# A transformer layer on eight cores: more load semaphores, and two kinds of store moved from ScalarE's DMA queue to SyncE's

## The reference

```
x = x + attn(layernorm(x)) @ wo.T        # causal softmax attention, q,k,v = h @ wq.T, wk.T, wv.T
g = silu(layernorm(x) @ w_gate.T)
u = layernorm(x) @ w_up.T
x = x + (g * u) @ w_down.T
```

## Time and profile before

| | us |
|---|---|
| median of 3 runs | 2900.47 (2899.7 to 2901.21) |
| profiled execution, its own time | 2899.5 |
| span of its slowest core (core 4), first to last instruction | 2897.1 |
| spans of the 8 cores | 2885.8 to 2897.1 |
| PE busy | 2449.2 (85%) |
| DVE busy, ACT busy | 557.8 (19%), 551.4 (19%) |
| DMA, mean over the span | 68 GB/s |

### The profile page before, as it was taken

How to read it: one execution, slowest core, us unless ns; L and a number is a source line. 1 busy time by engine, 2 the same in 40 slices (tenths; PEclk the granted TensorE clock), 3 DMA queues, 4 the chain that set the end, 5 groups by cost and what they waited for, 6 DMA issues and landing times.

```text
span 2897.1 us, 32038 instructions; the slowest of 8 cores (2885.8 to 2897.1 us)
## 1 busy us (share of the span) xinstructions
PE 2449.2 (85%) x12352; PEld 1142.4 (39%) x12352; DVE 557.8 (19%) x978; ACT 551.4 (19%) x1090; POOL 169.2 (6%) x324
## 2 busy tenths in 40 slices
PE   2676788888888888859879999999999999797886
PEld 1233344444444444414334444444444444343333
DVE  4322233333333333303210001000000000000000
ACT  4433223232333333302310000000000000000000
POOL 0000000000000000010000000000000011111110
PEclk9988999999999999958889999999999999898998
DMA  5433211101010101073234444444444435555554
GB/s 171 114 105 80 44 18 20 22 16 22 16 23 15 23 15 23 1 145 117 80 80 80 73 79 74 79 75 79 75 78 75 78 62 76 113 76 110 87 99 94
DMA packets 61491, 196.36 MB, mean 68 GB/s; under 512 B 6944, under 2 KB 6944, under 8 KB 56096
## 3 DMA queue, kind: packets, MB, share of 16 engines
q0 software_dynamic: 46080, 134.24, 28.5%
q1 hardware_dynamic: 9504, 43.29, 4.7%
q10 hardware_dynamic: 5760, 16.78, 1.5%
HBM read 311.72 MB, written 16.78 MB: 113 GB/s over the span
## 4 chain that ended last, share of the span: by engine, by line
PE 79%; ACT 7%; DMA 6%; issue 4%; DVE 4%; ACTq 0%; DVEq 0%; POOL 0%; SPq 0%; POOLq 0%
PE psA L717 8%; PE psB L728 8%; PE psA L394 4%; PE psA L414 4%; PE psA L802 4%; PE psB L394 4%; PE psB L414 4%; PE psF L728 4%; PE psE L728 4%; PE psC L717 4%; PE psD L717 4%; PE psB L802 4%; PE psB L331 2%; PE psA L331 2%; ACT p_sb L459 2%
## 5 line engine op out<-in xcount | busy, mean ns | idle before, releaser
L459 ACT ACTIVATE p_sb<-psA,stats 128x1024 bf16<-128x1024 f32 (+3 forms) x128 | 132.4, 1034 | 558.4 <-PE psA L443 290.5
L717 PE MATMUL psA<-h_fm,wg 128*128 128x512 bf16 x1024 | 227.9, 381 | 9.0 <-DMA wg<-wg_t 9.0
L728 PE MATMUL psB<-h_fm,wu 128*128 128x512 bf16 x1024 | 226.2, 379 | 0.0
L717 PE MATMUL psC<-h_fm,wg 128*128 128x512 bf16 x512 | 194.0, 379 | 0.0
L717 PE MATMUL psD<-h_fm,wg 128*128 128x512 bf16 x512 | 194.0, 379 | 0.0
L728 PE MATMUL psE<-h_fm,wu 128*128 128x512 bf16 x512 | 194.0, 379 | 0.0
L728 PE MATMUL psF<-h_fm,wu 128*128 128x512 bf16 x512 | 194.0, 379 | 0.0
L802 PE MATMUL psB<-wd,hidden 128*128 128x512 bf16 x512 | 155.4, 384 | 22.7 <-DVE osb L816 22.6
L802 PE MATMUL psA<-wd,hidden 128*128 128x512 bf16 x512 | 154.4, 382 | 5.6 <-DVE osb L816 3.8
L526 DVE CAST pt<-psD 128x512 bf16<-128x512 f32 x192 | 115.7, 603 | 210.2 <-PE psD L513 210.2
L717 PEld LDWEIGHTS psA<-h_fm,wg 128*128 128x128 bf16 x1024 | 100.5, 98 | 131.0 <-issue 11.4
(11 more groups left out here) (124 smaller groups left out, 2986.0 us busy)
## 6 DMA issues: line engine op xcount, KB each, us to landing
wg<-wg_t POOLq DMA_DIRECT2D x64, 512.0 KB, 5.1
wu<-wu_t POOLq DMA_DIRECT2D x64, 512.0 KB, 5.1
wd<-wd_t POOLq DMA_DIRECT2D x128, 256.0 KB, 3.8
xt<-xkv SPq DMA_DIRECT2D x16, 1024.0 KB, 5.7
wqbuf<-wq_t POOLq DMA_DIRECT2D x16, 512.0 KB, 5.1
xt<-xq SPq DMA_DIRECT2D x8, 1024.0 KB, 10.2
wkbuf<-wk_t POOLq DMA_DIRECT2D x16, 512.0 KB, 5.7
wvbuf<-wv_t POOLq DMA_DIRECT2D x16, 512.0 KB, 5.7
```

What stands on the lines that cost most here:

```text
L459: t_exp = P.do("scalar", lambda e, s=s, slo=slo, shi=shi, sec=sec, sc_t=sc_t, sstat=sstat: e.activation(sb["p_sb"][:, P_OFF[s] + slo:P_OFF ...
L717: t_gmm = P.do("tensor", lambda e, hc=hc, c=c, half=half, par=par, gb=gb: e.matmul(bk(gb[half]), wg[par][:, c, :], sb["h2_fm"][:, c, half ...
L728: t_umm = P.do("tensor", lambda e, hc=hc, c=c, half=half, par=par, ub=ub: e.matmul(bk(ub[half]), wu[par][:, c, :], sb["h2_fm"][:, c, half ...
```

## The change

Three edits. The groups `ld` and `wld` get six semaphores in place of four. The store of `x2t` (L651) is started by SP and no longer by ACT. So is the store of `osb` (L821).

```diff
-DMA_GROUPS = {"ld": 4, "wld": 4, "st": 2}
+DMA_GROUPS = {"ld": 6, "wld": 6, "st": 2}
...
-        x2st_tok[slot] = P.dma("scalar", lambda e, slot=slot, par=par: e.dma_start(
+        x2st_tok[slot] = P.dma("sync", lambda e, slot=slot, par=par: e.dma_start(
             out=dr["x2s"][slot * 128:(slot + 1) * 128, :], in_=x2t[par][:, :]),
             ev_toks, "st")
...
-            t_st = P.dma("scalar", lambda e, qtr=qtr, tt=tt, par=par: e.dma_start(
+            t_st = P.dma("sync", lambda e, qtr=qtr, tt=tt, par=par: e.dma_start(
                 out=dr["out"][tt * 128:(tt + 1) * 128, qtr * 512:(qtr + 1) * 512],
                 in_=osb[par][:, :]), [t_ev], "st")
```

## The result

The changed kernel took 2909.4 us (median of 12 runs) against 2899.8 for the kernel before beside it; the ratio is 1.003, with a 95% interval of 1.0019 to 1.004, so +8.7 us (+5.5 to +11.6). The forecast was 2903.6 us, +3.15 on the kernel before, with a range of 2896 to 2912. The time lies inside the range; the size of the change is near three times what I had worked out, and the interval leaves out no change at all, where I had forecast a cost too small to be told. Some executions of both kernels are disturbed and far longer (3240 us, say); the ratio leaves them out.

A forecast was written before the change was run, and what follows sets the result against it. PE bounds the kernel (79% PE, 6% DMA), so queues matter only where PE waits for transfers. Terms 0 + 0 + 0.75 + 0 + 2.4 = +3.15 us on 2899.5, plus 1.0 for the median: 2903.6 us, range 2896 to 2912.

The forecast's parts named there:

- rival A: The forecast itself: a small cost below what can be told, own range 2901 to 2906 us; chance 0.62.
- rival C: Stage 5 quarter ends: one queue serves store and load without overlapping latencies; slower, 2921 us, half of it 2911; chance 0.15.
- The six semaphores: Stage 3 `woT` loads: six in flight gain 0, as the DMA share has no gap; at most 18 us.
- The joint lists: Extra satisfied waits on POOL before `woT` and `wg` loads, and on PE after `wg`: +0.75 us, bounds 0.4 and 1.5.
- The first `xt` tile: Program start: DVE's 15.49 us wait for it stays 15.5, change 0; at most 3.7 us later.
- The store of `x2t`: Slots 2, 4, 6: the `xot` load moves behind the store on SP but lands in time; 0, upper bound 0.1.
- The store of `osb`: Stage 5 quarter ends: load starts 0.42 us later with 0.2 to spare; 12 rounds x 0.2 = +2.4 us.
- B: Stage 5 quarter ends: the store goes out first and quickly, the addition waits for the load alone; faster, 2894 us; chance 0.11.
- D: `xot` loads come late, slots 2, 4 and 6 push the following layer norm; +6 us, 2910; chance 0.05.
- E: Stage 3: deeper loading streams `woT` faster; a third of 18 us back gives 2898, all 2886; chance 0.05.
- 12 x 0.36 = 4.3 us: Stage 5 quarter ends: cost of the `osb` store's move by the skill's start-time rule, if no load had time to spare.
- the other rule, turns between queues: First rounds beside `wd` loads: one queue gets fewer DMA turns, 0.8 us might double at three quarter ends, +2.4 us.

The follow-up runs named there:

- e1_sems: Kernel before with only the six `ld` and `wld` semaphores, both stores still on ACT; ratio 1.0007 (0.9988 to 1.0026).
- e2_out: Kernel before with only the `osb` out store moved to SP, four semaphores, `x2s` store on ACT; ratio 1.0014 (0.9987 to 1.0042).
- the repeat: The changed kernel, all three edits, measured once more in another session against the kernel before; ratio 1.0032 (1.0008 to 1.0056).
- e3_x2s: Kernel before with only the store of `x2t` to `x2s` moved to SP; ratio 1.0007 (0.9996 to 1.0018).
- e4_loadfirst: Changed kernel with SP starting the next `x2r` load ahead of the out store, same queue; ratio to the kernel before 1.0003 (0.9989 to 1.0017).
- e5_late7: Kernel before, out store on ACT, with seven satisfied waits on SP ahead of each `x2r` load; ratio 1.006 (1.0018 to 1.0103).
- e6_late24: Kernel before, out store on ACT, with 24 satisfied waits on SP ahead of each `x2r` load; ratio 1.003 (0.9983 to 1.0077).

## Why the prediction was right or wrong

**Where it acts.** Right. The quarter ends changed, and the way that the text said: SP's load 0.43 us after the store (I had 0.42), DVE's waits put down to the load, though in all 24 cases and not in half. Of the signs that I had named, one failed: rounds two and three were to stay within half a us of before, and grew by 0.8 (5.48 to 6.29). The time is also outside the range of rival A itself, 2901 to 2906. It lies near the 2911 of half of rival C, whose mechanism did not come; that the range of 2896 to 2912 holds it is owed to the room left for that rival, and so in part to luck.

**The six semaphores.** Right. `woT` loads took 18.4 us to land (median) where they took 12.0, PE's wait for them stayed, and the DMA share in the window from 1280 to 1290 was what it was the earlier trace rows:

```profile
1280.00:1290.00 10.00, 6.17 (x14) 1.42 (x14) 0.00 (x0) 0.00 (x0) 1.58 (x3) 0.50 1.04 173
```

The joint lists: after `wg` had landed, PE took 1.22 us to its first matmul where it took 0.98, which is the predicted 0.25. POOL took 1.68 us from the last copy on ACT (end at 1468.89) to the start of the first `wg` load (1470.57), where it took 1.44; again 0.24. The single edits show the same: 1.22 and 1.68 in e1_sems, with six semaphores, 0.98 and 1.43 in e2_out, with four. The landing of `wg` in between scattered by more than that, 6.2 to 7.6 us over these four profiles, the repeat and e3_x2s. The first `xt` tile was waited for 15.9 us in e3_x2s as well, with four semaphores, so its 0.4 us is scatter. The rows:

```profile
1468.61 0.28 ACT h_fm L617
...
1470.08 0.49 issue
1470.57 7.40 DMA wg<-wg_t
1477.97 1.22 issue
```

**The store of `x2t`.** Right. The store of slot 1 was started at 1326.28 and the two `xot` loads behind it. The additions of slot 2 came 11.3 us later with the same wait for PE ahead of them as before, 3.79 us, and so did the reduction, 2.73 us. The load for slot 2 took 8.8 us from 1326.66 and was in at 1335.5, which is 9.2 after the store's start (I had 7.8, or 10.8 with the third megabyte) and 2.1 ahead of the addition:

```profile
1326.28 0.33 SPq L651 DMA_DIRECT2D x2s<-x2t  x1
1326.66 1.39 SPq L665 DMA_DIRECT2D xot<-xq  x2
...
1337.59 1.29 DVE L644 TENSOR_TENSOR x2t<-psA,xot 128x512 f32<-128x512 f32 x2 [3.79 <-PE psD L613]
...
1342.80 2.29 DVE L252 TENSOR_REDUCE stats<-x2t 128x1 f32<-128x2048 f32 x1 [2.73 <-PE psD L613]
```

**The store of `osb`.** The mechanism was right, and this term was mis-sized: "so 0.42 - 0.2 = 0.2 us for each round, if the DMA engines spend the time they did before: 12 x 0.2 = 2.4 us". Measured were 84.1 - 79.4 = 4.7 us, and 83.8 - 79.4 = 4.4 in the repeat, but 81.8 - 79.4 = 2.4 with this edit alone. Taken together, the three profiles with the out store on SP have a mean of 83.2, and the three with both transfers started together (before, e1_sems, e3_x2s) 79.6: 3.6 us, with a standard error of 0.9. The sum alone therefore does not exclude my 2.4. The rounds do show that it was put together wrongly, and the condition in the sentence is what failed. Over all cores in rounds two and three, the store landed 4.56 us after its start before and the load after 4.34, so the 0.2 to spare was right. Once second, the load starts 0.44 later and also takes longer, 4.87; the store takes 4.02. That is 0.44 + 0.53 - 0.22 = 0.75 us a round, and 0.81 was measured. What the load loses, 0.53, the store gains, 0.54, and nobody waits for the store.

The first rounds went the other way where weight loads run beside them. At the three inner quarter ends they became shorter, from 7.5 to 7.3 us for the even tiles and from 8.2 to 8.0 for the odd ones (7.1 and 7.9 in the repeat, 7.0 and 7.8 in e2_out). At the last quarter end, where there are none, they became longer, from 5.6 to 6.4 and from 6.3 to 7.1. So the cost is not 12 equal rounds, and why it turns round beside the weight loads stays open.

**From a typical core to the slowest of eight.** The sum left this step out. The mean span rose by 5.7 us in the first measurement and by 4.6 in the repeat, about the quarter ends plus 0.75; the time rose by 8.7, and with its interval by 5.5 to 11.6. The four-quarter sums of the eight cores lay within 7.1 us of one another before and within 10.8 after, but also within 10.7 in e3_x2s, whose time did not change. So the wider spread is not shown to be the cause of the rest; this stays open.

**The rivals.** B (stores first, faster) did not come: the store did become faster, and the addition waited for the load. C (one queue without overlap, +9.8 to +20) is excluded by e4_loadfirst, which has both transfers on one queue at no cost, and by e5_late7, which has the cost on two. D and E are excluded by the waits above. The Trainium skill's rule (DMA: Bandwidth & Descriptors, Rules for kernel authors), that separate queues save only the time of starting because all run on the same engines, agrees with e4_loadfirst, where one queue cost nothing. The 12 x 0.36 = 4.3 us that I worked out by it cannot be told from my own 2.4 by the measured 3.6 with its standard error of 0.9. It is near for a reason that it does not have: it counts 0.36 in every round, where rounds two and three grew by 0.8 and the inner first rounds became shorter. What I had worked out from the other rule, turns between queues, was a longer first round beside the weight loads; the measured ones are shorter.

## What to carry to other kernels

Where a wait ends with the later of two transfers, try both orders: here, on one and the same queue, the load first gave a sum of 78.3 us and the store first 84.1 and 83.8. A start that was 0.44 us late cost 0.8 us in each of rounds two and three, because the late transfer also took longer to land. A round that repeats on the critical path multiplies such a figure. Rather than tune such a round, look whether a free stretch of memory lets it go: eight buffers for two were worth 1.8 to 2.8% here, and then the queue did not matter (the order was not tried). More `woT` loads in flight brought nothing, with a DMA share of 1.04: each landed after 18.4 us instead of 12.0, and the wait of PE stayed.

## What the runs showed of the hardware that I had not expected

A satisfied wait on SP that repeats the same semaphore took 0.05 us, near the 0.06 on POOL. The cost of a late start is nearly flat once it is there: with the load 0.4 us behind the store (e5_late7) rounds two and three took 6.42 us, with 1.7 us on the mean (e6_late24) 6.54, against 5.48 with both started together, since the later load landed 1.2 us sooner (3.85 against 5.03). And two 256 KB transfers on one queue, the load first, landed after 4.2 and 4.3 us (e4_loadfirst, mean of the eight cores' medians), sooner than the same pair started together on two queues (4.7 and 4.8).
